# Rounding the gate and up weights during in_proj, and turning all feed-forward weights by transposing DMA

## The reference

```
x = x + mamba(layernorm(x))          # in_proj 1024 -> 2 x 2048, conv, scan over 512 steps, out_proj
x = x + cross(layernorm(x), context) # both operands fake-quantised to 8 bits, one matmul
x = x + ffn(layernorm(x))

def fake_quant(t, axis):             # in ffn: one scale per row, codes -128..127
    s = max(max(|t|, axis) / 127, 1e-8)
    return clip(round(t / s), -128, 127) * s
def qlinear(x, w): return fake_quant(x) @ fake_quant(w, axis=1).T
def ffn(x):
    h = silu(qlinear(x, w_gate)) * qlinear(x, w_up)   # w_gate, w_up: 2752 x 1024
    return qlinear(h, w_down)                         # w_down: 1024 x 2752
```

## Time and profile before

| what | value |
|---|---|
| median of 3 runs | 1796.08 us |
| profiled execution, its own time | 1802.02 us |
| its span, first to last instruction | 1800.2 us |
| TensorE busy | 1454.5 us (81%) |
| VectorE busy | 1388.2 us (77%) |
| ScalarE busy | 860.6 us (48%) |
| GpSimd busy | 967.6 us (54%) |
| mean granted TensorE clock | 0.923 |

### The profile page before, as it was taken

The page is one execution under the profiler, slowest core; times in us unless marked ns, Lnnn a source line. Parts: engine busy times, 40 slices in busy tenths (PEclk is TensorE's granted clock), DMA queues, the critical chain, the costliest instruction groups (busy, mean ns, idle before and its releaser), DMA issues. The chain is left out here.

```text
span 1800.2 us, 18744 instructions
## 1 busy us (share of the span) xinstructions
PE 1454.5 (81%) x5912; PEld 771.3 (43%) x5912; DVE 1388.2 (77%) x1748; ACT 860.6 (48%) x1213; POOL 967.6 (54%) x793
## 2 busy tenths in 40 slices
PE   5998667778688877577877888888999479999788
PEld 3443333444344443443434444443444245555333
DVE  4423898998998998989989889972674758889684
ACT  1212555565565446556456455541422357878200
POOL 0001968788878787988878978951000002222530
PEclk8999789889989989679999999998999779999889
DMA  4243211331321321314624615635710234342004
GB/s 152 92 165 122 83 60 52 126 107 36 127 101 40 122 70 36 106 59 151 194 71 171 203 47 200 195 151 193 265 47 36 82 133 175 130 171 100 24 0 164
DMA packets 73676, 205.15 MB, mean 114 GB/s; under 512 B 6800, under 2 KB 24336, under 8 KB 68784
## 3 DMA queue, kind: packets, MB, share of 16 engines
q1 hardware_dynamic: 70416, 188.29, 30.4%
q10 hardware_dynamic: 3168, 15.73, 2.4%
HBM read 176.66 MB, written 27.33 MB: 113 GB/s over the span
## 5 line engine op out<-in xcount | busy, mean ns | idle before, releaser
L931 DVE TENSOR_TENSOR_SCAN hbuf<-decay,hbuf 128x512 f32<-128x512 f32 x512 | 614.0, 1213 | 73.2 <-ACT decay L661 73.2
L499 PE MATMUL turn<-ident,hbuf 128*128 128x128 f32 x2048 | 342.1, 299 | 226.8 <-DVE hbuf L931 174.4
L661 ACT ACTIVATE decay<-delta,chan_sb 128x512 f32<-128x512 f32 x512 | 349.6, 689 | 304.8 <-DVE hbuf L931 303.4
L499 PEld LDWEIGHTS turn<-ident,hbuf 128*128 128x128 f32 x2048 | 261.1, 153 | 507.7 <-DVE hbuf L931 255.3
L945 DVE SCALAR_TENSOR_TENSOR acc<-turn,pn,acc 128x512 f32<-128x512 f32 x360 | 263.2, 731 | 19.6 <-PE turn L499 17.9
L789 POOL TENSOR_TENSOR acc<-acc,part 128x512 f32<-128x512 f32 x120 | 152.8, 1273 | 25.6 <-ACT part L671 25.6
L1793 POOL TENSOR_TENSOR hid<-gs,us 128x512 f32 (+1 forms) x44 | 56.3, 1285 | 194.6 <-ACT gs L1753 179.0
L770 POOL TENSOR_TENSOR hbuf<-du,b_more 128x512 f32<-128x512 f32 x128 | 158.9, 1276 | 0.0
L770 POOL TENSOR_TENSOR hbuf<-wout,sx 128x512 f32<-128x512 f32 x128 | 158.6, 1272 | 0.4 <-POOL wout L778 0.2
L770 POOL TENSOR_TENSOR hbuf<-wout,b_more 128x512 f32<-128x512 f32 x128 | 158.7, 1274 | 0.0
L770 POOL TENSOR_TENSOR hbuf<-du,sx 128x512 f32<-128x512 f32 x128 | 158.4, 1269 | 0.0
(11 more groups left out here) (208 smaller groups left out, 2175.6 us busy)
## 6 DMA issues: line engine op xcount, KB each, us to landing
wout<-in_woutT SPq DMA_DIRECT2D x48, 512.0 KB, 4.2
codes<-in_wg SPq DMA_DIRECT2D x8, 2048.0 KB, 7.9
sx<-bt_scratch SPq DMA_DIRECT2D x64, 256.0 KB, 3.2
b_more<-bt_scratch SPq DMA_DIRECT2D x64, 256.0 KB, 3.2
raw_d<-in_w_down SPq DMA_DIRECT2D x8, 1376.0 KB, 5.7
wout<-in_w_gate SPq DMA_DIRECT2D x21, 512.0 KB, 3.9
wout<-in_w_up SPq DMA_DIRECT2D x21, 512.0 KB, 4.8
wout<-in_wu SPq DMA_DIRECT2D x18, 512.0 KB, 3.5
```

The costliest lines, as they stand in the source:

```text
L499: last = pe.transpose(turn[t % 2][:, j * P:j * P + P], hbuf[:, s % 4, j, t * P:t * P + P], ident[:, :])
L661: act.activation(decay_bank[q % 2][:, :], delta[:, G % 2, j, :], ACT.Exp, scale=a_col(GD * (G % GROUPS) + j, n)).then_inc(dA_done, 1)
L931: dve.tensor_tensor_scan(h, decay_bank[q % 2][:, :], h, 0.0, ALU.mult, ALU.add).then_inc(scan_done, 1)
```

## The change

**mixer.** The 22 chunks of gate and up rows (44 units of up to 128 x 1024) are rounded while in_proj runs. SyncE loads a unit to one of six buffers, VectorE takes its row maxima and scales, ScalarE scales and adds the rounding constant, GpSimd subtracts it and writes bfloat16 codes to one of three buffers, and SyncE stores them in `wq_dram`. `pairs_at` gives the chunk pairs of each step: one or two of them, in 15 steps.

**attend.** It no longer rounds anything. After the last out_proj product it loads the codes of the first four chunks by transposing DMA.

**feed_forward.** The ring of turned weights has four places, filled by transposing DMA from `wq_dram`. TensorE turns nothing. w_down is rounded as before, its codes made plain on GpSimd and turned by a transposing DMA from SBUF to SBUF, one for each tile of 128 rows. The products use banks 0 to 3 and 4 to 7 in turn. In the down projection the rounding of batch 1 goes from VectorE to ScalarE, in two instructions.

```diff
@@ mixer, sync
+            def load_raw(u):
+                m, c, n = u % 2, u // 2, unit_rows(u)
+                if u >= RAWS:
+                    sp.wait_ge(w_code, u - RAWS + 1)
+                else:
+                    sp.wait_ge(stat, 4 * (u + 1))
+                sp.dma_start(raw[u % RAWS][0:n, :], (w_gate, w_up)[m][c * P:c * P + n, :]).then_inc(raw_in[u % RAWS], 16)
+            def store_code(u):
+                m, c, n = u % 2, u // 2, unit_rows(u)
+                sp.wait_ge(w_code, u + 1)
+                sp.dma_start(wq_dram[m, c * P:c * P + n, :], wcode[u % CODES][0:n, :]).then_inc(w_stored[u % CODES], 16)
...
+        def pairs_at(i):
+            return range(OC * i // PREPS, OC * (i + 1) // PREPS) if 0 <= i < PREPS else range(0)     # PREPS = 15
...
+            for u in range(RAWS):
+                load_raw(u)
             for g in range(GROUPS):
                 for j in range(GD):
-                    load_w(2 + GD * g + j)
+                    i = GD * g + j
+                    load_w(2 + i)
+                    if g >= 1 and j == 2:
+                        load_wx(g)
+                    for c in pairs_at(i - 1):
+                        for u in (2 * c, 2 * c + 1):
+                            store_code(u)
+                        for u in (2 * c + RAWS, 2 * c + RAWS + 1):
+                            if u < UNITS:
+                                load_raw(u)
...
+            for i in range(CODES):
+                sp.wait_ge(w_stored[i], all_stored(i))
             load_u(0)
@@ mixer, scalar
+            def weight_round(c):
+                act.wait_ge(w_scale, 4 * c + 5)
+                for m in range(2):
+                    u = 2 * c + m
+                    v = raw[u % RAWS][0:unit_rows(u), :]
+                    act.activation(v, v, ACT.Identity, bias=rnd[0:unit_rows(u), 0:1],
+                                   scale=keep.iw[0:unit_rows(u), m, c:c + 1]).then_inc(w_round, 1)
...
             for i in range(2, DC):
                 conv_first(i)
+                for c in pairs_at(i - 2):
+                    weight_round(c)
+                if i == DC - 1:
+                    for c in pairs_at(i - 1):
+                        weight_round(c)
                 if i % GD == GD - 1:
                     u_silu(i // GD)
@@ mixer, gpsimd (ahead of rms(0))
+            for u in range(UNITS):
+                pool.wait_ge(w_round, u + 1)
+                if u >= CODES:
+                    pool.wait_ge(w_stored[u % CODES], stored_before(u))
+                n = unit_rows(u)
+                pool.tensor_scalar(wcode[u % CODES][0:n, :], raw[u % RAWS][0:n, :], -ROUND, None, ALU.add).then_inc(w_code, 1)
@@ mixer, vector
                     if GD * g + j >= 2:
                         conv_rest(GD * g + j)
+                        for c in pairs_at(GD * g + j - 2):
+                            weight_scales(c)      # two tensor_reduce, tensor_scalar, reciprocal
+                        if GD * g + j == DC - 1:
+                            for c in pairs_at(DC - 2):
+                                weight_scales(c)
@@ attend, sync
-            for c in range(AHEAD):
-                for m, w in enumerate((w_gate, w_up)):
-                    sp.dma_start(keep.raw[:, c, m, :], w[c * P:c * P + P, :]).then_inc(raw_in, 16)
+            for c in range(WT):
+                for m in range(2):
+                    sp.dma_start(keep.wT[:, c, m, :, :], wq_dram[m, c * P:c * P + P, :], transpose=True).then_inc(wT_in, 16)
@@ feed_forward, sync
+            def load_wT(c):
+                sp.wait_ge(up_mm, 2 * (c - WT) + 2)
+                r = rows(c)
+                for m in range(2):
+                    sp.dma_start(wT[:, c % WT, m, :, 0:r], wq_dram[m, c * P:c * P + r, :], transpose=True)\
+                        .then_inc(wT_load[c % WT], 16)
+            def turn_wd(t):
+                sp.wait_ge(wd_plain, NP * (t + 1))
+                sp.dma_start(wdT[:, 0:OC, t * P:t * P + P], code_d[:, :], transpose=True).then_inc(wd_turned, 16)
@@ feed_forward, tensor
             def products(c):
+                if c >= WT:
+                    pe.wait_ge(wT_load[c % WT], 32 * (c // WT))
                 for b in range(BATCH):
                     for m, (banks, free, done) in enumerate(...):
-                        if c >= 1:
-                            pe.wait_ge(free, 2 * (c - 1) + b + 1)
+                        if c >= 2:
+                            pe.wait_ge(free, 2 * (c - 2) + b + 1)
+            for c in range(OC):
+                products(c)
@@ feed_forward, scalar and vector, down projection
+            for c in range(OC):
+                v = hid[0:r, c, L:2 * L]
+                act.wait_ge(q_scaled[1], c + 1)
+                act.activation(v, v, ACT.Identity, bias=rnd[0:r, 0:1]).then_inc(q_rounded, 1)
+                act.wait_ge(q_rounded, c + 1)
+                act.activation(to, v.unsqueeze(1), ACT.Identity, bias=rnd[0:r, 1:2]).then_inc(q_done[1], 1)
...
                 scale_hid(before + 1)
-                for b in range(BATCH):
-                    dve.wait_ge(q_done[b], before + 1)
-                    hid_codes(before + 1, b, q_space(before, b))
+                dve.wait_ge(q_done[0], before + 1)
+                hid_codes(before + 1, 0, q_space(before, 0))
```

More of the change, by code:

```diff
@@ L28 @@
 LN_EPS, RMS_EPS = 1e-5, 1e-6
-AHEAD = 2
+WT = 4
 QMAX, SMIN = 127.0, 1e-8
@@ L100, in mixer @@
                   for i in range(TOK // P)]
+        RAWS, CODES = 6, 3
+        ubuf_rows = ubuf[1][:, :, :].rearrange("p j t -> p (j t)")
+        raw = [acc[:, i // 2, 2 * (i % 2):2 * (i % 2) + 2, :].rearrange("p t d -> p (t d)") for i in range(4)] + \
+              [ubuf_rows[:, 0:H], ubuf_rows[:, H:2 * H]]
+        wcode = [part[:, 0, :].bitcast(BF16), part[:, 1, :].bitcast(BF16), y_out[:, 0, :].bitcast(BF16)]
         conv_w = chan_sb[:, C_CONVW:C_CONVB].rearrange("p (c k) -> p c k", k=TAPS)
@@ L667, in scaled_state @@
                 act.wait_ge(turned, bank_turn(G, n, ZT))
+                if k <= 2:
+                    for i in range(2):
+                        act.wait_ge(w_stored[i], all_stored(i))
                 if k >= 3:
@@ L1470, in _, with feed_forward @@
                     context_code(k)
-def feed_forward(nc, keep, w_gate, w_up, w_down, x2_dram, out):
+def feed_forward(nc, keep, wq_dram, w_down, x2_dram, out):
     NT = TOK // P
@@ L1674, in products @@
                         for k in range(KC):
[L1675 removed]
+                            last = pe.matmul(banks(c, b)[0:r, :], wT[:, c % WT, m, k, 0:r], keep.codes[:, k, b * L:b * L + L],
                                              start=(k == 0), stop=(k == KC - 1))
                         last.then_inc(done, 1)
[L1679 to L1687 removed]
@@ L1798, in scale_hid, with plain @@
                 pool.tensor_tensor(v, v, ih_row[0:r, L:2 * L].unsqueeze(1), ALU.mult).then_inc(q_scaled[1], 1)
-            with pool.Fori(0, OC - 1) as c:
-                for b in range(BATCH):
-                    multiply(c, b)
-            for b in range(BATCH):
-                multiply(OC - 1, b, OLAST)
+            def plain(t, m):
+                pool.wait_ge(wd_code, NP * t + m + 1)
+                if m == 0 and t >= 1:
+                    pool.wait_ge(wd_turned, 16 * t)
+                pool.tensor_scalar(code_d[:, piece(m)], raw_d[:, piece(m)], -ROUND, None, ALU.add).then_inc(wd_plain, 1)
+            pool.memset(code_d[:, INTER:OC * P], 0.0).then_inc(pad_made, 1)
+            for c in range(OC + 1):
+                if c >= 1:
+                    for b in range(BATCH):
+                        multiply(c - 1, b, rows(c - 1))
+                if c - 1 in wd_at:
+                    for m in range(NP):
+                        plain(wd_at[c - 1], m)
             pool.wait_ge(ih_kept, 2)
```

289 lines of the change are left out of this document (99 added, 190 removed).

## The result

The changed kernel took 1938.69 us (median of 4 runs, 1937.05 to 1941.12) against 1795.60 for the kernel before (4 runs). The ratio is 1.080, with a 95% interval from 1.078 to 1.082. The forecast was 1844: the direction is right, but the loss is 143 us where 48 were forecast.

What follows compares the result with a forecast made beforehand. In_proj was taken as TensorE-bound, the feed-forward as nearly full on TensorE, VectorE and ScalarE. Terms +140 (in_proj stage), -2, -84.5 and -6 gave +47.5 on 1796.1, so 1844 us; own range 1807 to 1874, full range 1795 to 1950.

Steps and rivals of the forecast that it cites:

- In_proj's stage, +137 forecast: In in_proj, weight loads wait behind the rounding chain in SyncE's queue; last ssm product starts at 297.3 against 160.2 us.
- the first wait: In in_proj, chunks 4 and 5 wait for the first pairs' codes; group start 98.2 against 77.8 us, +20.4.
- The last stretch: End of in_proj: from the last group's start at 240.0 through products 14 and 15 to the last ssm product at 297.3.
- The prediction's high end for the stage: In in_proj, +170 us with GpSimd's code at 2.6 us, weight landings of 6.5 and a cold TensorE clock.
- Rival 1: In in_proj, rounding hides in idle engine time; last ssm product at 189.5, kernel faster at 1733 us; chance 0.14.
- Products of the feed-forward, -84.5 forecast: Feed-forward: TensorE's turns and their PSUM copies go; 22 chunks at 6.91 us plus cold start, 154.9 against 239.4 us.
- none of these is late at 6.91: Feed-forward: with two bank sets, VectorE, ScalarE and GpSimd keep up with TensorE's 6.91 us a chunk.
- no dearer: Feed-forward, VectorE: the two peaks a chunk cost no more than before, within 5.6 us a chunk.
- the sign that it set itself: Feed-forward: the forecast counts as wrong if the chunk pitch is over 8 us.
- Rival 2: Feed-forward: transposing DMA is slow; at 81 GB/s a chunk takes 10.9 us, the 84.5 are gone, 1928 us; chance 0.25.
- End of attention, -2 forecast: Attention's end: roundings of chunks 0 and 1 go, -2 us (0 to 2.7); turning loads hidden; cold projection turns add 3.
- Down projection, -6 forecast: Down projection: VectorE's step falls from three instructions to two, 4.5 to 3.0 us, beside GpSimd; -6 us (0 to -20).

Runs made afterwards that it cites:

- e0: Kernel before, plus eleven extra GpSimd instructions on an unused buffer while GpSimd had no work in in_proj, to measure prices; 1802.87 us.
- e2: Changed kernel with in_proj's code step split: GpSimd takes the first 512 columns of a unit, ScalarE the other 512; 1922.52 us.
- e1: Changed kernel with in_proj's weight loads of chunks 4 to 17 issued from ScalarE's queue instead of SyncE's; 1842.90 us.
- e8: e7 with the last pair of roundings of each in_proj product put behind the next bias copy on ScalarE; 1803.11 us.
- e11: e10 with the loads of wx and of the gate's first weights one product earlier in SyncE's order; 1773.00 us, ratio 0.9875 to the kernel before.
- e3: Changed kernel without load, maxima, rounding and codes of w_down tiles 1 to 7 (tile 0 turned eight times, layer not computed); 1886.06 us.
- e6: Changed kernel with GpSimd's codes made by a cast of each rounded float's low 16 bits, in in_proj and feed-forward; 1887.61 us.
- e5: Changed kernel with the next w_down tile's load issued ahead of the transposing DMA of the tile before; 1931.20 us.
- e7: Changed kernel with the edits of e1, e5 and e6 together; 1814.37 us.
- e10: e8 with group-end loads and last silu moved earlier, plus a w_down tile's three ScalarE roundings spread over half chunks; 1788.03 us, ratio 0.9953 to the kernel before.
- e4: Changed kernel with the last step of w_down's codes in the feed-forward done by ScalarE instead of GpSimd; 1937.32 us.

## Why the prediction was off in size

**In_proj's stage, +137 forecast, +171.5 measured: mechanism right, one duration mis-sized and one load left out.** The prediction took 1.6 us for GpSimd's `tensor_scalar` of 1024 columns, from the affine select as the nearest one-input row; the trace shows 2.77, and e0 shows it alone. Four of them stand in the chain, twice a group. Four times 1.17 is 4.7 us; the load went out 19.5 us after the bias copy (100.69 to 120.18) where 15.1 was worked out, and landed after 5.6, later ones after up to 6.9 (5.4 forecast). A group took 80.4 us against 70.9 forecast, so two groups give 19 of the missing 34 us and the first wait 2.4. The last stretch gives 12.7: the load for product 14 also stands right behind the gate's first weights, 2 MB that the prediction left out of SyncE's order. The two issues:

```profile
281.33 0.43 SPq L318 DMA_DIRECT2D codes<-in_wg  x1
281.80 0.43 SPq L279 DMA_DIRECT2D wout<-in_wu  x1
```

That load landed 11.2 us after its issue (product 14 at 292.95), where the others took 5.6 to 6.9, and it was issued 4.9 later after the bias copy than worked out, again for the codes. The prediction's high end for the stage, +170 with 2.6 us and landings of 6.5, was the better estimate, and it is right partly by luck, as it has nothing for the 2 MB load. How much of the 34 us the code's price alone is worth, e2 shows: with loads going out at the forecast's 15.1 the stage is 15 us shorter and still 19 too long. Those 19 are the landings, the 2 MB load and what that edit itself adds on ScalarE, and were not separated. The slip is in how it chose between bounds. The affine select takes 0.29 us for 128 columns, 2.3 ns a column taken whole; the 1.44 came from taking off a fixed part that a memset had given. The two-operand add, with 512 columns and 2.5 ns each, was the row nearest in size.

**Rival 1 (the rounding hides) fell** on the ground named against it, the order in the queues. e1, e8 and e11 are its measure: with the order mended and the cheaper code the last ssm product starts at 195.09 (e11), near the rival's 189.5, and the kernel is faster than before.

**Products of the feed-forward, -84.5 forecast, -22.5 measured: the step that failed.** The prediction said "none of these is late at 6.91" after adding up each engine's busy time a chunk (VectorE 5.6 us, GpSimd 4.0). For TensorE this holds, and e3 shows 153.9 us for the chunks alone. For the engines behind it it does not quite: the peak, put at "no dearer", takes 1.40 us beside GpSimd's multiplication where it took 0.69 before, and the ring of VectorE and ScalarE passes a chunk in 7.0 us. But a tile of `w_down` is a chain with one buffer: load, maxima, rounding, codes, transposing issue, and then the next load. The prediction priced the pieces and never laid them in order of time, although it had done just that for the roundings of in_proj. By the sign that it set itself (a pitch over 8 us a chunk) it was wrong: the pitch is 9.4. The trace gives a tile 28.2 us where three chunks' ring takes 21.0. The 7.1 us more, read from VectorE's lines between the halves, are 4.1 where it waits for the landing (2.05) and takes the maxima, 2.4 behind ScalarE's three roundings, and some 0.6 net from GpSimd's 7.61 us ahead of two multiplications (one half 0.7 shorter, as its peak has no multiplication beside it, and the next 1.3 longer). So the products end 194.1 us after the first load (1801.8), 40 more than in e3. The wait behind the last product, until VectorE has passed the last tile, is 23.9 us, where the prediction kept the 1.0 of before: 23 more. That is the 62 us that are missing. Some 9 of them stand in e3 too (9.9 us of wait without tiles) and belong to the ring; the rest are the tiles'. The experiments take the chain apart: e6 (codes) 2.5 us a tile, e5 (issue order) 2.2, both together (e7) no more than 2.5, e10 (the roundings' burst) 2.7 more. e4 says why the sum of busy time misleads: ScalarE had room for the work, but not at that place in the ring.

**Rival 2 (the transposing DMA is slow) comes near the measured time, 1928, by coincidence.** It lost all of the 84.5 us in the feed-forward, where 62 went, and had nothing of the 34 lost in in_proj. It put the old pace of 10.9 us a chunk down to bandwidth; the pace is 9.4, for another reason. The transposing loads did their part, 32 products every 7.0 us in e3. That is 512 KB in 7.0 us, at least 75 GB/s. The Trainium skill, "DMA: Bandwidth & Descriptors", section "Latency and other measured facts", with its 261 GB/s, is not contradicted by this, and not shown either. The price of a single block in the Trainium skill, "VectorE: DVE Perf Modes", section "The three transpose paths", can't be taken once for each block here: the estimated 31 us a chunk are more than four times the 7.0 of e3. What they cost is SyncE's time: 3.3 us for each issue of the 704 KB one, 6.7 where a load goes ahead of it.

**End of attention, -2 forecast:** from the last ssm product to the feed-forward's first load the kernel is 7.8 us shorter, where -2 +3 was worked out. The eight turning loads are hidden, as said. Where the other 9 us come from was not settled: with the scan alone, from its first turn (190.89, then 363.88) to that load, the changed kernel takes 1243.8 against 1253.2 us, and the experiments that hold the change lie between 1240.7 and 1247.8. VectorE's scans took 1.209 instead of 1.213 us in the middle of the stage, which is too little to explain it. The only other trace with the old kernel's scan, e0's, has 1253.1 as well, but both are of executions 6 or 7 us above that kernel's median, so part of the 9 us may be those executions and not the change. No run was made for this.

**Down projection, -6 forecast, -5.0 measured.** VectorE's step is now of two instructions, and beside GpSimd one starts every 3.08 us (the next at 1851.64):

```profile
1848.56 1.75 DVE L1890 TENSOR_TENSOR hid<-hid,wout 128x512 f32 x1
1850.47 1.25 DVE L1894 TENSOR_SCALAR hid<-hid  x1 [0.16 <-DVE hid L1890]
```

The 1.5 us for each instruction that the prediction read from the earlier trace rows holds, so the number of instructions set the pace while GpSimd scales, as it said.

## What to carry to other kernels

Idle shares of 60% say nothing while one queue in order serves both the old work and the new: write down what each queue issues between two of the old loads, small and rare loads too, and give the loads on the path a queue on which nothing waits for the new work. Lay a chain with one buffer out in order of time before adding up busy shares, and place its pieces one at a time in the gaps of the ring they share, since a burst of 3.2 us costs 2.7 us a tile where its three pieces, of at most 1.2, cost nothing. Price an operation that no row shows at its own size, or take both bounds for the sum; one short instruction put at 1.6 us stood four times in a chain.

## What the runs showed of the hardware

GpSimd's operation with a scalar immediate took 2.77 us for 1024 columns and 1.49 for 512 (some 0.2 us fixed, 2.5 ns a column), 1.5 times an add of two operands (1.89, both the same tile) and 2.7 times a cast (1.04), with a strided 16-bit input as cheap as a plain one. VectorE's add of 512 columns took 1.40 us beside GpSimd's two-operand multiplication and 0.69 beside its operation with a scalar. A 512 KB load issued right behind a 2 MB load on one queue landed after 11.2 us against 5.6 to 6.9. A transposing DMA of 704 KB from SBUF kept SyncE's queue for 3.2 to 3.8 us, and for 6.7 with a 1.4 MB load issued right ahead of it. After 19 to 31 us of idle time a product of 16 matmuls took 8.5 to 9.9 us where 7.03 is usual, and the granted clock over 60 to 331 us was 0.72, against 0.88 over 60 to 235 us in e1, whose TensorE waits less.
